# Clearing attention tiles slot by slot, deferring stores, and issuing the rows of the maxima from GpSimd

## The reference, cut to what matters

```python
Q, K, V = heads(ln(x) @ Wq + bq), heads(ln(x) @ Wk + bk), heads(ln(x) @ Wv + bv)
scores  = einsum('bhqd,bhkd->bhqk', Q, K) / 4 + mask      # |i-j|<=64, or i==0, or j==0
x = x + (softmax(scores) @ V merged) @ Wo + bo
x = x + experts(ln(x)) + shared(ln(x))                    # 16 experts, top 512 rows each
```

## Time and profile before

| | |
|---|---|
| runs | 1281.91, 1283.11, 1285.75 us; median 1283.11 |
| profiled execution | 1284.79 us; span from first to last instruction 1282.8 us |
| mean granted clock of TensorE | 0.955 of full |
| busy in the span | PE 1158.4 us (90%), DVE 854.4 (67%), POOL 630.6 (49%), ACT 597.9 (47%) |
| queue q1 | 50592 packets, 130.71 MB |
| queue q0 | 12352 packets, 16.92 MB |

### The profile page before, as it was taken

The page is one execution under the profiler, slowest core; times in us unless marked ns, Lnnn a source line. Parts: engine busy times, 40 slices in busy tenths (PEclk is TensorE's granted clock), DMA queues, the critical chain, the costliest instruction groups (busy, mean ns, idle before and its releaser), DMA issues. The chain is left out here.

```text
span 1282.8 us, 23570 instructions
## 1 busy us (share of the span) xinstructions
PE 1158.4 (90%) x8906; PEld 969.1 (76%) x8906; DVE 854.4 (67%) x2182; ACT 597.9 (47%) x961; POOL 630.6 (49%) x792
## 2 busy tenths in 40 slices
PE   0997799989999549999985999999999999999997
PEld 0885577766677349987874788888888888888886
DVE  7895677767777057747876766666677666766641
ACT  1341466656666425432222555545455555545442
POOL 8000356656565426411001476666666676677654
PEclk9997699989999868999997999999999999999999
DMA  2589477777775376210132444444444444444311
GB/s 92 183 292 133 151 119 126 129 128 131 129 122 97 90 189 191 66 54 34 35 114 80 150 120 111 132 106 109 132 129 125 125 104 127 103 127 127 92 29 17
DMA packets 63053, 149.08 MB, mean 116 GB/s; under 512 B 15168, under 2 KB 32064, under 8 KB 53728
## 3 DMA queue, kind: packets, MB, share of 16 engines
q1 hardware_dynamic: 50592, 130.71, 39.3%
q0 software_dynamic: 12352, 16.92, 7.8%
HBM read 104.73 MB, written 42.34 MB: 115 GB/s over the span
## 5 line engine op out<-in xcount | busy, mean ns | idle before, releaser
L611 DVE CUSTOM_DVE_ANT_0 junk_s<-ps_s,mask 128x258 bf16<-128x258 f32 (+2 forms) x512 | 212.6, 470 | 91.8 <-PE ps_s L692 91.0
L1852 POOL TENSOR_TENSOR held<-h,held 128x512 fp32r<-128x512 f32 x128 | 178.4, 1406 | 124.0 <-ACT held L1888 123.8
L665 ACT ACTIVATE pt<-ps_p 128x516 f32<-128x516 f32 (+2 forms) x256 | 167.1, 680 | 82.0 <-PE ps_p L713 67.6
L1962 PE MATMUL ps_gu<-xt_hi,w_hi 128*128 128x512 f32 x512 | 203.3, 397 | 2.1 <-DVE xt_lo L1911 2.1
L1962 PE MATMUL ps_gu<-xt_lo,w_hi 128*128 128x512 f32 x512 | 200.2, 391 | 0.0
L1962 PE MATMUL ps_gu<-xt_hi,w_lo 128*128 128x512 f32 x512 | 200.0, 391 | 0.0
L1927 DVE TENSOR_TENSOR h<-ge,ps_gu 128x512 f32<-128x512 f32 x128 | 87.9, 686 | 165.1 <-ACT ge L1882 141.1
L1790 DVE TENSOR_TENSOR w_lo<-w,w_hi 128x768 fp32r<-128x768 f32 x128 | 174.7, 1369 | 31.1 <-ACT w_hi L1785 27.6
L498 POOL TENSOR_SCALAR_AFFINE_SELECT pt<-pt 128x256 f32<-128x256 f32 x352 | 133.0, 417 | 119.8 <-ACT pt L665 119.6
L1979 PE MATMUL ps_y<-w_hi,held 128*128 128x256 f32 x1024 | 187.9, 282 | 3.4 <-ACT stage L1898 1.7
L692 PE MATMUL ps_s<-ks,qs 96*128 96x258 f32 (+2 forms) x512 | 157.3, 364 | 9.3 <-PEq L198 9.1
(11 more groups left out here) (198 smaller groups left out, 2140.5 us busy)
## 6 DMA issues: line engine op xcount, KB each, us to landing
w<-in_We SPq DMA_DIRECT2D x48, 1024.0 KB, 4.9
qk_parts<-held SPq DMA_DIRECT2D x8, 2064.0 KB, 7.8
qs<-qk_parts SPq DMA_DIRECT2D x96, 129.0 KB, 4.2
ks<-qk_parts SPq DMA_DIRECT2D x96, 129.0 KB, 5.6
x<-in_x SPq DMA_DIRECT2D x16, 512.0 KB, 7.9
attn_t<-on SPq DMA_DIRECT2D x32, 256.0 KB, 5.9
ot<-attn_t SPq DMA_DIRECT2D x16, 256.0 KB, 4.6
rd<-rden SPq DMA_DIRECT2D x16, 256.0 KB, 4.1
```

The costliest lines, as they stand in the source:

```text
L611: dve.tensor_tensor_reduce(junk[:, (u * SG + g) % RING, 0:n], ps_s[:, (u * SG + g) % RING, 0:n], m, 1.0, -3e38, ALU.add, ALU.max, mx[:, u ...
L665: act.activation(dst, src, ACT.Exp, scale=SCALE).then_inc(exp_s, 1)
L1852: pool.tensor_tensor(h_lo[:, m], h32[:, (e * KI + m) % HB], h_hi[:, m].bitcast(F32), ALU.subtract).then_inc(hlo_s, 1)
L1962: last = pe.matmul(ps_gu[:, m % 2, n], l, r, start=c == 0, stop=c == 3 * KD - 1)
```

## The change

One: POOL clears slot 0 only at the start (`fill(0)`, two memsets over one slot, `ks` all 1.0), and slots 1 to 4 in front of the copies of batches 1 to 4; the casts of mask and identity move to batch 5. SP waits for the fills by their own semaphore. Two: the store of batch 7 leaves `project` and becomes SP's first act in `attend`. Three: `m_rows` moves from SP to POOL, where it stands behind `take_v(u)`, and the first one behind `negated(1)`. Four: `far_rows` moves behind the seventh exponential. Five: SP waits for the landing of the reciprocals only before the next `load_den`, and stores them at t = 0 of the batch after.

```diff
 (project, SP)
-                sp.wait_ge(ready, 4)
+                sp.wait_ge(fill_s, 2 * SL)
                 for u in range(SL):
                     sp.wait_ge(out_s[u // UB % 2], (u // UB // 2 + 1) * 16)
                     load_step(sp, d, ks, qs, qk_in, u)
                 step(B // 2 - 1, 0, False)
-                step(B // 2 - 1, 1, False)
 (project, POOL)
-                pool.memset(qs[:].bitcast(F32), 0.0).then_inc(ready, 1)
-                pool.memset(ks[:].bitcast(F32), 0.0).then_inc(ready, 1)
-                pool.memset(ks[M_ROW:M_ROW + 2].bitcast(F32), 1.0).then_inc(ready, 1)
...
+                def fill(place):
+                    pool.memset(qs[:, place].bitcast(F32), 0.0).then_inc(fill_s, 1)
+                    pool.memset(ks[:, place].bitcast(F32), 1.0).then_inc(fill_s, 1)
+                fill(0)
                 for b in range(B):
+                    if 1 <= b < SL:
+                        pool.wait_ge(xn_s, b + 1)
+                        fill(b)
+                    if b == SL:
+                        (casts of mask and ident16)
                     pool.wait_ge(qlo_s, b * 4 + 4)
 (attend, POOL)
+                def m_rows(u):
+                    t = u % SL
+                    pool.wait_ge(mt_s, u + 1)
+                    if u == 0:
+                        pool.wait_ge(qk_in[0], 16 * LOADS)
+                    rows = qs[M_ROW:M_ROW + 2, t].bitcast(F32).rearrange("c h (j i) -> c (h j) i", j=NT)
+                    for k in range(MK):
+                        pool.dma_start(rows[:, :, 32 * k:32 * k + 32], mt[32 * k:32 * k + 32, u % 2]).then_inc(m_in[t], 16)
...
                 negated(1)
+                m_rows(0)
                 for u in range(NU):
                     take_v(u)
+                    if u + 1 < NU:
+                        m_rows(u + 1)
                     near_only(u, 1)
 (attend, SP)
+                    if b >= 1:
+                        sp.wait_ge(rden_out, b * 16)
                     src = d["ot"][b].rearrange(...)   # load_den
...
-                    sp.wait_ge(rden_out, b * 16 + 16)  # store_rden
...
-                m_rows(0)
+                sp.dma_start(d["qk"][B - 1]..., qk[:, 1]...).then_inc(qk_out[1], 16)
                 for u in range(NU):
-                    if u + 1 < NU:
-                        m_rows(u + 1)
...
-                    if b >= 1 and t == 3:
-                        store_rden(b - 1)
+                    if b >= 2 and t == 0:
+                        store_rden(b - 2)
+                store_rden(B - 2)
 (attend, ACT)
+                        if n == 6 and u + 1 < NU:
+                            far_rows(u + 1)
                         if n == 6 and u >= 1:
                             out_rows(u - 1)
-                        if n == 5 and u + 1 < NU:
-                            far_rows(u + 1)
```

More of the change, by code:

```diff
@@ L123, in build @@
         project(nc, d, sem, tally, ident, bias, eps, ks, qs, v, mask, ident16, qk_in, qk, qk_out)
-        attend(nc, d, sem, tally, ks, qs, v, mask, ident16, qk_in, qk_out, held, stage)
+        attend(nc, d, sem, tally, ks, qs, v, mask, ident16, qk_in, qk, qk_out, held, stage)
         att.close()
@@ L180, in project @@
         whi = sem("p_whi")
+        fill_s = sem("p_fill")
         ready = sem("p_ready")
@@ L233, in _ @@
                 pool.memset(eps[:], EPS).then_inc(ready, 1)
-                pool.wait_ge(ready, 1)
-                pool.memset(qs[:].bitcast(F32), 0.0).then_inc(ready, 1)
-                pool.wait_ge(ready, 2)
-                pool.memset(ks[:].bitcast(F32), 0.0).then_inc(ready, 1)
-                pool.wait_ge(ready, 3)
-                pool.memset(ks[M_ROW:M_ROW + 2].bitcast(F32), 1.0).then_inc(ready, 1)
[L241 to L247, removed]
-                for b in range(B):
+                def fill(place):
+                    pool.memset(qs[:, place].bitcast(F32), 0.0).then_inc(fill_s, 1)
+                    pool.memset(ks[:, place].bitcast(F32), 1.0).then_inc(fill_s, 1)
+                fill(0)
+                for b in range(B):
+                    if 1 <= b < SL:
+                        pool.wait_ge(xn_s, b + 1)
+                        fill(b)
+                    if b == SL:
+                        pool.wait_ge(m_in, 16)
+                        pool.tensor_copy(mask[:], m32[:]).then_inc(ready, 1)
+                        pool.wait_ge(i_in, 16)
+                        pool.tensor_copy(ident16[:], ident[:]).then_inc(ready, 1)
                     pool.wait_ge(qlo_s, b * 4 + 4)
@@ L417, in load_step, with attend @@
             sp.dma_start(dst[n * DH:(n + 1) * DH, u % SL].bitcast(F32), d["qk"][u // UB, part, u % UB]).then_inc(qk_in[u % SL], 16)
-def attend(nc, d, sem, tally, ks, qs, vs, mask, ident16, qk_in, qk_out, held, stage):
+def attend(nc, d, sem, tally, ks, qs, vs, mask, ident16, qk_in, qk, qk_out, held, stage):
     with ExitStack() as ctx:
@@ L541, in _ @@
             def _(sp):
[L542 to L548, removed]
                 def store(u):
@@ L575, in load_piece @@
                         sp.dma_start(staged(c), d["Sw"][:, PIECE * (c - 1):PIECE * c]).then_inc(piece_in, 16)
-                m_rows(0)
+                sp.dma_start(d["qk"][B - 1].rearrange("c (m t) d h q -> (t d h) c m q", m=KD),
+                             qk[:, 1].rearrange("p c m k i -> p c m (k i)").bitcast(F32)).then_inc(qk_out[1], 16)
                 for u in range(NU):
                     b, t = u // UB, u % UB
-                    if u + 1 < NU:
-                        m_rows(u + 1)
                     if 1 <= u <= NU - SL:
@@ L593, in _ @@
                         load_den(b - 1)
-                    if b >= 1 and t == 3:
-                        store_rden(b - 1)
+                    if b >= 2 and t == 0:
+                        store_rden(b - 2)
+                store_rden(B - 2)
                 store(NU - 2)
                 store(NU - 1)
+                sp.wait_ge(rden_out, (B - 1) * 16)
                 sp.wait_ge(bo_in, 16)
```

## The result

1267.57 us median (1267.00 to 1269.56, 4 runs) against 1282.51 (1281.70 to 1285.75, 4 runs): ratio 0.988, 95% interval 0.986 to 0.990. The change is faster by 15 us, which is 1.2% and clear of the scatter; 31 were forecast, and the time lies just above the range. The profiled span went from 1282.8 to 1265.5 us, 17.3 less; that is 2.4 more than the medians give, as the profiled execution of the kernel before (1284.79 us) was 2.3 us above its median.

The account below looks back on a forecast made before the run. PE was taken as full except for holes behind POOL's memsets, the barrier, the first rows and late rows; 19.2 + 7.9 + 2.0 + 3.0 = 32.1 us off 1284.79 gives 1252.7, corrected to the median 1251 us; range 1240 to 1266.

Parts of the forecast that it names:

- Fills: At the start, clearing slot 0 only lets PE begin at 9.2 us instead of 28.41: gain 19.2 us.
- Barrier: Between `project` and `attend`, moving batch 7's store frees the barrier from SP's stalled queue: gain 7.9 us.
- Start of the rows: Before the first exponents, POOL's rows land at 131.2 us, PE follows at 131.5: gain 2.0 us beyond the barrier.
- The rule of turns between queues: At the first rows, DMA engines alternate between queues by packet, so 4 KB don't wait for two 2 MB stores.
- Rows in each step: In 31 attention steps, POOL-issued rows arrive in time: 10.2 less 4.6 and 2.6 us returned, net gain 3.0 us.
- the 10.2 us of excess: Time of the 31 attention steps above 8.89 us each before the change; all forecast to go.
- rival 2: In the attention, rows late every step with landing 4.3 us; attention loses 5.6 instead of winning 3.0: 1260 us; 17%.
- `far_rows`: Between the seventh exponential and PE's next exponents, its later place costs 0.15 us a step, 4.6 us in all.
- POOL's subtraction behind a piece of weights: In five attention steps POOL first subtracts for 1.82 us, delaying rows: cost 2.6 us, bounds 0 and 5.3.
- SP's waits: SP no longer held for the landing of the reciprocals' store: cost and further gain nothing.

Follow-up runs that it names:

- e1: The kernel before with only the fills in pieces, `fill(b)` as in the change; 1265.72 us, 0.986 of before.
- e4: The changed kernel with the store of batch 7 back at the end of the first block; 1285.27 us (1 run).
- e2: The changed kernel with all rows of the maxima issued by SP again, first in its step; 1254.42 us, 0.976 of before.
- e6: The changed kernel with rows of steps 0 and 1 from POOL, the rest from SP, and `far_rows` back behind the sixth exponential; 1245.61 us.
- e9: The changed kernel without SP's `load_step` inside the attention, rows still from POOL, output not the reference's; 1251.47 us (1 run).
- e8: The changed kernel with rows from SP after steps 0 and 1, and reciprocals stored at t = 3 and waited for at once; 1257.30 us.
- e11: e6 with `m_rows(0)` on POOL moved in front of `negated(1)`; 1244.10 us, 0.969 of before.
- e10: The changed kernel with rows of steps 1 to 31 issued by ACT behind its second exponential, into ACT's own queue; 1259.63 us (1 run).

## Why the prediction was wrong
**Fills: right.** 19.2 forecast, 19.2 found, nothing lost in later slots. The cause is shown by e1.
**Barrier: right.** 7.9 forecast; 8.0 by e4 (98.11 against 90.11).
**Start of the rows: the size was off.** 2.0 forecast beyond the barrier; of the 28.4 us of the start, 27.7 were there before the first score, so the rows gave 0.6. The rule of turns between queues in the page "DMA: Bandwidth & Descriptors" of the Trainium skill, section "Queues, rings and completion order", held in this, that the rows did not stand behind the two stores: e2, whose rows do, starts 8.5 us later. But turns are not free: the first rows of the changed kernel landed after 5.1 us in the median, where I took 3.2.
**Rows in each step: wrong, and this is the step that failed.** I wrote "the rows are in time by 0.8 us, and the 10.2 us of excess go", with a landing of 3.2 us from the nearest row, and leaned to a shorter one for the pieces, as the transfer is sixteen times smaller. For the same 4 KB the landing is 1.9 us with the DMA engines nearly idle and 4.6 beside the loads, so the size alone does not set it. Against my 3.2 the 4.6 is 1.4 us more; POOL's quicker issue, three slots of 0.6 instead of 0.8, gives 0.6 back, and the 0.8 us in hand is used up in the median step. With landings up to 7.3 us, 21 steps wait. Instead of 10.2 regained, 11.3 more were lost. It was rival 2, whose 4.3 us landing was nearly right; its price of 5.6 us was half the true 11.3, as I let each step be late by its mean and forgot that a long wait lowers the clock for the next step. I had both numbers for it: 0.76 of the engines busy, and a landing of 5.4 us.
**`far_rows`: the size.** 4.6 us forecast, 1.6 found (e6). The 2.6 us for POOL's subtraction behind a piece of weights have no run of their own; in e9, with a landing of 1.9 us, the whole excess is 0.1.
**SP's waits: I put nothing down for them alone**, and gave the whole 10.2 us to the rows' issuer. e8 shows that the deferred wait by itself is worth 8.7 us of steps, and e2 that with it SP issues every row in time. The 10.2 were not all the rows' either: 5.3 of them are the step of 14.23 us, in which ACT waited for a piece of weights, and the list of rows' waits does not show it. The two edits mended the same stall: the deferred wait was enough, and the other cost 21.6 us of steps.
By the page "DMA: Bandwidth & Descriptors" of the Trainium skill, section "Issuing engines are not separate DMA queues", transfers of all issuers share the same 16 engines, and spreading them saves only issue time. On the sharing e9 against the changed kernel agrees, with a landing of 1.9 us against 4.6.

## What to carry to other kernels
In this kernel the small transfer on the critical path did best ahead of the bulk in the queue that carries the bulk; a queue of its own helped only where the bulk was already queued, as with the first rows. Before moving it, look why the queue it is in was late: here a wait of its issuer for a store that nobody needed yet. And price a landing by how busy the DMA engines are at that moment, not by its size.

## What the runs showed of the hardware
- 4 KB transfers issued by POOL cost it 0.60 us each and landed after 1.9 us (median, e9) with the DMA engines 0.17 busy, 4.6 us (changed kernel) at 0.69, and 7.0 us (e11, first rows) at 1.00.
- The same transfers in SP's queue, ahead of the loads, had landed within 3.4 us in most steps (e6, engines 0.73 busy); in ACT's queue, beside the loads, four took 5.3 to 5.7 us (e10).
- Four `tensor_scalar` from SBUF to SBUF on DVE took 20.51 us beside POOL's memsets, 19 more than otherwise, and were not held at all by fills that lie between them (e1).
- In one PE idle of 2.82 us, in a stretch where the engine had been full, the granted clock fell to 0.50; it stayed there until about 192 us, and the step that followed took 4.95 us more (changed kernel).
